# Turning the quantised activations with VectorE blocks and a trip through DRAM, where TensorE transposed them

## The reference

```python
def fp4_quant_dequant(x):
    xb = x.reshape(shape[:-1] + (shape[-1] // BLOCK, BLOCK))      # BLOCK = 16
    scale = jnp.maximum(jnp.max(jnp.abs(xb), axis=-1, keepdims=True) / 6.0, 1e-12)
    xn = xb / scale
    return (_GRID[jnp.searchsorted(_MID, jnp.abs(xn))] * jnp.sign(xn) * scale).reshape(shape)

gate, y = fp4_linear(x, w_gate), fp4_linear(x, w_up)              # 256 -> 704
return fp4_linear(jax.nn.silu(gate) * y, w_down)                  # 704 -> 256
# whole: x + attn(xn) + ffn(xn), xn = layernorm(x)
```

## Time and profile before

| | |
|---|---|
| median of three runs | 2815.54 us |
| the profiled execution: its time | 2811.82 us |
| its span, first to last instruction | 2810.2 us |
| PE busy | 2577.6 us, 92% |
| ACT busy | 2034.4 us, 72% |
| DVE busy | 1936.9 us, 69% |
| POOL busy | 687.3 us, 24% |
| granted TensorE clock, mean | 0.970 |

### The profile page before, as it was taken

How to read it: one execution, slowest core, us unless ns; L and a number is a source line. 1 busy time by engine, 2 the same in 40 slices (tenths; PEclk the granted TensorE clock), 3 DMA queues, 4 the chain that set the end, 5 groups by cost and what they waited for, 6 DMA issues and landing times.

```text
span 2810.2 us, 60356 instructions
## 1 busy us (share of the span) xinstructions
PE 2577.6 (92%) x18236; PEld 1313.6 (47%) x18236; DVE 1936.9 (69%) x5533; ACT 2034.4 (72%) x3510; POOL 687.3 (24%) x478
## 2 busy tenths in 40 slices
PE   2995998898889859999999999999999999999999
PEld 1883444444444424444454445445444445444445
DVE  6895998898889865656655665655566564656555
ACT  1554887897889857777766777775777775777775
POOL 3563233323232212111111211211121121212211
PEclk8997999999999989999999999999999999999999
DMA  2785544444454442122123022031221231220200
GB/s 68 234 269 119 78 61 67 69 67 69 67 70 67 62 78 45 32 33 46 28 63 72 22 41 47 22 69 58 33 49 26 34 69 54 45 47 22 41 24 31
DMA packets 117099, 175.52 MB, mean 62 GB/s; under 512 B 24880, under 2 KB 93232, under 8 KB 116272
## 3 DMA queue, kind: packets, MB, share of 16 engines
q1 hardware_dynamic: 97392, 147.33, 27.9%
q10 hardware_dynamic: 16576, 15.73, 2.1%
q0 software_dynamic: 2816, 8.91, 1.1%
HBM read 129.37 MB, written 42.53 MB: 61 GB/s over the span
## 4 chain that ended last, share of the span: by engine, by line
PE 53%; ACT 4%; issue 4%; DMA 1%; SPq 1%; DVE 0%; ACTq 0%; POOL 0%; DVEq 0%; POOLq 0%
PE O L918 17%; PE S L902 15%; PE F L938 10%; PE F L978 5%; ACT probs L1047 4%; PE F L968 2%; PE S L989 2%; PE S L905 2%; SPq L528 1%; PE F L931 1%; DMA y<-in_L_attn_x_dram 1%; DMA q_st<-s_shift 0%; ACTq L1042 0%; DVE o_turned L1253 0%; DVE ht_lo L1241 0%
## 5 line engine op out<-in xcount | busy, mean ns | idle before, releaser
L1047 ACT ACTIVATE probs<-S 128x1024 f32<-128x1024 f32 (+3 forms) x1280 | 1074.7, 897 | 213.7 <-PE S L902 77.3
L744 DVE CUSTOM_DVE_ANT_0 m_excess<-m_S,m_excess 128x512 f32<-128x512 f32 (+7 forms) x1536 | 702.3, 531 | 58.8 <-ACT m_excess L723 38.3
L723 ACT ACTIVATE m_excess<-m_DIFF 128x512 f32<-128x512 f32 (+7 forms) x1536 | 640.5, 473 | 124.8 <-PE m_DIFF L676 36.1
L902 PE MATMUL S<-q_st,k_st 128*128 128x512 bf16 (+3 forms) x2560 | 648.3, 351 | 65.7 <-DMA q_st<-s_shift 28.7
L918 PE MATMUL O<-probs,v_sb 128*32 128x512 f32 (+3 forms) x5120 | 602.3, 542 | 1.7 <-POOL v_sb L1124 1.7
L676 PE MATMUL m_DIFF<-m_k,m_q_diff 128*128 128x512 bf16 (+7 forms) x1536 | 489.9, 326 | 61.0 <-DMA m_q_diff<-s_q 29.8
L676 PE MATMUL m_S<-m_k,m_q 128*128 128x512 bf16 (+7 forms) x1536 | 492.1, 330 | 18.5 <-DVE m_row_max L744 10.6
L902 PEld LDWEIGHTS S<-q_st,k_st 128*128 128x128 bf16 x2560 | 213.4, 98 | 407.8 <-ACT probs L1047 236.3
L631 POOL TENSOR_TENSOR m_q_diff<-m_zero,m_q 48x4096 bf16<-48x4096 bf16 x32 | 224.3, 7011 | 519.6 <-DMA m_q<-s_q 508.5
L676 PEld LDWEIGHTS m_S<-m_k,m_q 128*128 128x128 bf16 x1536 | 150.4, 98 | 257.5 <-DVE m_row_max L744 181.3
L1241 DVE TENSOR_TENSOR ht_lo<-F,ht_hi 128x512 fp32r<-128x512 f32 (+1 forms) x128 | 71.0, 558 | 232.0 <-ACT ht_hi L1062 232.0
(11 more groups left out here) (163 smaller groups left out, 4167.9 us busy)
## 6 DMA issues: line engine op xcount, KB each, us to landing
k_st<-s_k SPq DMA_DIRECT2D x96, 256.0 KB, 8.5
q_st<-s_q SPq DMA_DIRECT2D x384, 64.0 KB
s_q<-a_part SPq DMA_DIRECT2D x48, 256.0 KB, 3.0
s_k<-a_part SPq DMA_DIRECT2D x48, 256.0 KB, 2.2
m_q<-s_q SPq DMA_DIRECT2D x96, 128.0 KB, 3.6
m_k<-s_k SPq DMA_DIRECT2D x96, 128.0 KB, 6.4
m_q_diff<-s_q SPq DMA_DIRECT2D x96, 128.0 KB, 7.9
m_k<-s_k SPq DMA_DIRECT2D x96, 124.0 KB, 5.1
```

The source lines that it names most:

```text
L723: act.activation(excess[u % MAX_EXCESS][:, 0:keys // 2], DIFF[u % MAX_BUFS][:, 0:keys // 2], ACT.Relu) \
L744: dve.tensor_tensor_reduce(larger, S[u % MAX_BUFS][:, 0:keys // 2], larger, 1.0, -3e38, ALU.add, ALU.max, column).then_inc(reduced[u % MAX ...
L902: ins = pe.matmul(S[half][:, s % 2, 0:st.width], k_st[p][:, s, st.j * P:(st.j + 1) * P], q_st[st.c % 2][:, s, st.skip:QC], start=True, sto ...
L1047: act.activation(probs[half][st.n % 2][:, :, 0:st.width], S[half][:, :, 0:st.width], ACT.Exp, scale=SCALE).then_inc(exped[half], 1)
```

## The change

Four edits, all in the main phase.

1. The turns. The transposes on PE (`x_turn`, `h_turn`) go. DVE transposes `x_fp4` and `h_fp4` in 32x32 blocks with one instruction each, into `x_flip` and `h_flip` (`h_flip` is also the buffer of `h_norm`). SP stores that to DRAM (128x256 and 128x768 float32), waits for the store, and loads it back with `unflip`: four DMAs, each for 32 partitions, whose contiguous pieces are 32 floats (128 bytes). That puts each block in its place, so `xt` and `ht` in SBUF are the transposed tiles.
2. ACT makes `xt_hi` at k=0 and `ht_hi` at k=9, now one instruction of 768 columns, from SBUF. POOL makes `xt_lo` and `ht_lo`.
3. SP's program is written out for the whole batch, with its loads in the order of the steps: the load of q for the next chunk stands where a chunk begins, ahead of `turn_h` where both are at k=4. The loads of the next batch's first tiles and v come at the end of a batch, v last.
4. After the steps: `h_turn` on DVE at m=2, `down` at m=12. At a batch's start `place_v` on POOL stands behind `x_rescale`.

```diff
-GATED_AT = {0: ("turn", 0), 2: ("gate", 0), 3: ("up", 0), 5: ("gate", 1), 6: ("up", 1)}
-GATED_FIRST_AT = {2: ("turn", 0), 4: ("gate", 0), 5: ("up", 0), 7: ("gate", 1), 8: ("up", 1)}
+GATED_AT = {0: ("high", 0), 2: ("gate", 0), 3: ("up", 0), 5: ("gate", 1), 6: ("up", 1)}
+GATED_FIRST_AT = {2: ("high", 0), 4: ("gate", 0), 5: ("up", 0), 7: ("gate", 1), 8: ("up", 1)}
+def unflip(eng, dst, dram, tiles, sem):
+    blocks = dram.rearrange("(a r) (m g s) -> g r m a s", r=SLOT, s=SLOT, g=P // SLOT)
+    for g in range(P // SLOT):
+        rows = dst[g * SLOT:(g + 1) * SLOT, :].rearrange("r (m a s) -> r m a s", m=tiles, s=SLOT)
+        eng.dma_start(rows, blocks[g]).then_inc(sem, 16)
+UNFLIP_DMAS = P // SLOT
...
+            def load_chunk(b, chunk):
+                hg, c = divmod(chunk, NQC)
+                if c == 0:
+                    load_stack(sp, k_st[hg % 2][:, :, :], dram["k"], K_STACK, hg * HG, HG, bass.ds(b * T, T), group_ld[hg % 2])
+                q = q_st[c % 2]
+                tokens = bass.ds(b * T + c * QC, QC)
+                sp.wait_ge(q_zeroed, 2)
+                sp.wait_ge(o_free[c % 2], b * (chunks // 2) + chunk // 2 + PRIMED)
+                load_stack(sp, q[:, :, :], dram["q"], Q_STACK, hg * HG, HG, tokens, q_ld[c % 2])
+                sp.dma_start(q[STACK:QK_ROWS, :, :],
+                             dram["shift"][:, bass.ds(b * H + hg * HG, HG), c * QC:(c + 1) * QC]) \
...
+                sp.wait_ge(q_zeroed, 2)
+                sp.wait_ge(v_ready, b * NHG + PRIMED)
+                sp.dma_start(v_in[:, :, :], dram["v"][:, bass.ds(b * NKB, NKB), :]).then_inc(v_ld, 16)
+            def turn_x(b, n):
+                sp.wait_ge(q_zeroed, 2)
+                sp.wait_ge(x_flipped, b * tiles + n + 1 + PRIMED)
+                sp.dma_start(dram["x_flip"], x_flip[:, :]).then_inc(x_flip_st, 16)
+                sp.wait_ge(q_zeroed, 2)
+                sp.wait_ge(x_flip_st, b * (16 * tiles) + 16 * (n + 1) + PRIMED)
+                unflip(sp, xt, dram["x_flip"], KD, xt_ld)
+            def turn_h(b, n):
+                sp.wait_ge(q_zeroed, 2)
+                sp.wait_ge(h_flipped, b * tiles + n + 1 + PRIMED)
+                sp.dma_start(dram["h_flip"], h_flip[:, :]).then_inc(h_flip_st, 16)
+                sp.wait_ge(q_zeroed, 2)
+                sp.wait_ge(h_flip_st, b * (16 * tiles) + 16 * (n + 1) + PRIMED)
+                unflip(sp, ht, dram["h_flip"], ITILES, ht_ld)
+            def batch(b, more):
+                turn_x(b, 0)
+                for st in steps:
+                    n, k = divmod(st.n, per_tile)
+                    if st.first and st.chunk + 1 < chunks:
+                        load_chunk(b, st.chunk + 1)
+                    if k == 4 and n >= 1:
+                        turn_h(b, n - 1)
+                    elif k == 6 and n + 1 < tiles:
+                        turn_x(b, n + 1)
+                if more:
+                    load_chunk(b + 1, 0)
+                turn_h(b, tiles - 1)
+                if more:
+                    load_batch(b + 1)
...
+            def down(b, n):
+                pe.wait_ge(ht_lo_done, b * tiles + n + 1 + PRIMED)
+                if n + 1 < tiles:
+                    pe.wait_ge(gated_done, b * 2 * tiles + 2 * (n + 2) + PRIMED)
                 else:
-                    pe.wait_ge(gate_free, b * 2 * tiles + 2 * n + 1 + PRIMED)
-                gated_product(0, "gate", ch, gate_ps)
...
                     if k == 0 and n >= 2:
                         down(b, n - 2)
-                    if op == "turn":
-                        x_turn(b, n)
-                    elif op == "gate":
+                    if op == "gate":
                         gate(b, n, ch)
                     elif op == "up":
                         up(b, n, ch)
-                    elif k in (8, 9) and n >= 1:
-                        h_turn(b, n - 1, k - 8)
                 down(b, tiles - 2)
                 values(b, steps[-1])
                 for m in range(tiles):
-                    if m == FLUSH_TURN:
-                        for part in range(2):
-                            h_turn(b, tiles - 1, part, flush=True)
-                    elif m == FLUSH_DOWN:
+                    if m == FLUSH_DOWN:
                         down(b, tiles - 1)
                     project(b, m)
...
+            def x_high(b, n):
+                act.wait_ge(xt_ld, b * (16 * UNFLIP_DMAS * tiles) + 16 * UNFLIP_DMAS * (n + 1) + PRIMED)
+                act.wait_ge(up_ps, b * 2 * tiles + 2 * n + PRIMED)
+                act.activation(xt_hi[:, :], xt[:, :], ACT.Copy).then_inc(xt_hi_done, 1)
+            def h_high(b, n):
+                act.wait_ge(ht_ld, b * (16 * UNFLIP_DMAS * tiles) + 16 * UNFLIP_DMAS * (n + 1) + PRIMED)
+                act.wait_ge(down_ps, b * tiles + n + PRIMED)
+                act.activation(ht_hi[:, :], ht[:, :], ACT.Copy).then_inc(ht_hi_done, 1)
             with act.Fori(0, B) as b:
                 for st in steps:
                     op, ch = gated_op(n, k)
                     exps(b, st, 0)
                     exps(b, st, 1)
-                    if op == "turn":
-                        act.wait_ge(xt_ps, b * tiles + n + 1 + PRIMED)
-                        act.activation(xt_hi[:, :], F[0][:, 0:KD * P], ACT.Copy).then_inc(xt_hi_done, 1)
+                    if op == "high":
+                        x_high(b, n)
                     elif op == "gate":
                         gate_parts(b, n, ch)
-                    elif k in (8, 9) and n >= 1:
-                        h_high(b, n - 1, k - 8)
+                    if k == 9 and n >= 1:
+                        h_high(b, n - 1)
                     if k == 9 and n + HEAD_TILES < tiles:
                         if n == 0:
                             act.wait_ge(y_st, b * (16 * (len(STORES) - 1)) + PRIMED)
                         load_tile(b, n + HEAD_TILES)
-                for part in range(2):
-                    h_high(b, tiles - 1, part)
+                h_high(b, tiles - 1)
                 for first, last in STORES:
                     store(b, first, last)
             act.wait_ge(y_head_st, 16 * B + PRIMED)
...
+            def x_low(b, n):
+                pool.wait_ge(xt_hi_done, b * tiles + n + 1 + PRIMED)
+                pool.tensor_tensor(xt_lo[:, :], xt[:, :], xt_hi[:, :].bitcast(F32), ALU.subtract).then_inc(xt_lo_done, 1)
+            def h_low(b, n):
+                pool.wait_ge(ht_hi_done, b * tiles + n + 1 + PRIMED)
+                pool.tensor_tensor(ht_lo[:, :], ht[:, :], ht_hi[:, :].bitcast(F32), ALU.subtract).then_inc(ht_lo_done, 1)
...
                 x_rescale(b, 0)
+                place_v(b, 0)
                 for st in steps:
                     n, k = divmod(st.n, per_tile)
+                    if gated_op(n, k)[0] == "high":
+                        x_low(b, n)
                     if k == 1:
                         add_bias(b, n)
                         if n + 1 < tiles:
                         x_rescale(b, n + 1)
                     elif k == 8:
                         h_normalise(b, n)
+                    elif k == 9 and n >= 1:
+                        h_low(b, n - 1)
                     if st.c == NQC - 1 and st.j == NKB // 2 and st.hg + 1 < NHG:
                         place_v(b, st.hg + 1)
                 h_rescale(b, tiles - 1)
+                h_low(b, tiles - 1)
...
+                def x_turn(n):
+                    dve.wait_ge(x_ready, b * tiles + n + 1 + PRIMED)
+                    dve.wait_ge(xt_lo_done, b * tiles + n + PRIMED)
+                    dve.transpose(x_flip[:, :], x_fp4[:, :]).then_inc(x_flipped, 1)
+                def h_turn(n):
+                    dve.wait_ge(h_ready, b * tiles + n + 1 + PRIMED)
+                    dve.wait_ge(ht_lo_done, b * tiles + n + PRIMED)
+                    dve.transpose(h_flip[:, :], h_fp4[:, :]).then_inc(h_flipped, 1)
...
                 x_scales(0)
                 x_round_(0)
+                x_turn(0)
                 for st in steps:
                     n, k = divmod(st.n, per_tile)
                     if k == 0:
                         if n >= 2:
                             add_down(n - 2)
-                        x_low(n)
                     elif k == 1 and n + 1 < tiles:
                         x_scales(n + 1)
                     elif k == 2 and n >= 1:
                         h_round_(n - 1)
                     elif k == 3:
                         gate_chunk(n, 0)
-                    elif k == 4 and n + 1 < tiles:
-                        x_round_(n + 1)
+                    elif k == 4:
+                        if n + 1 < tiles:
+                            x_round_(n + 1)
+                        if n >= 1:
+                            h_turn(n - 1)
                     elif k == 6:
                         gate_chunk(n, 1)
+                        if n + 1 < tiles:
+                            x_turn(n + 1)
                     elif k == 7:
                         h_scales(n)
```

(11 more changed lines are left out.)

114 lines of the change are left out of this document (35 added, 79 removed).

## The result

The changed kernel takes 2971.66 us (median; the kernel before beside it 2816.18): ratio 1.0552, 95% interval 1.0536 to 1.0568, so 155 us slower. The forecast was 2868, 52 slower. Its profiled span is 2958.3 us against 2810.2.

What follows compares the result with a forecast made beforehand. The prediction took PE to bound the kernel, with 1.18 us of transposes a tile on its path. 2811.8 us, +35 inside batches and +18 between them gave 2865, or 2868 for the median; range 2808 to 2990.

Steps and rivals of the forecast that it cites:

- the gain of h's turn: At `down`: k=9's scores start 0.59 us earlier, but the gain is spent on the low part, leaving x's 0.22.
- r=0: Tiles with n mod 4 = 0: q's load stands ahead of h's trip, so `down` is late; +0.8 us each.
- r=2: Tiles with n mod 4 = 2: h's trip stands behind q's load, `ht` 2.1 us late; +2.0 us each.
- The low part: Before `down`: ACT's copy 0.80, POOL's subtraction 1.51 and handovers 0.15, so 2.45 us behind k=9's last exponential.
- r=1 and 3: Tiles with n mod 4 = 1 or 3, no q load at k=4: `ht` in time with 2 us to spare, -0.2 us each.
- The four together: Tiles inside batches, by n mod 4: costs and gains sum to +8.8 us a batch, +35 over four batches.
- Between batches: Joints, first start and last end: 5.0 us at each of three joints, about +1 and +1.7 at the ends; +18.
- Rival A: DRAM trips: 128-byte pieces slow or ring full, a trip 8.7 us or more; 2920, or beyond 2990; chance 0.28.
- B: DRAM trips: always hidden; 2818 if all are, 2842 at a trip of 6.1 us; chance 0.13.
- C, the other side: At `down`: ACT so far ahead that h's parts finish during `values`, so the gain stays; 2774 us; chance 0.10.
- D: At `down`: something else paces it, as the q load at tile 4, absorbing lateness; within the forecast's range; chance 0.04.
- The start of the reading: Chain of waits over the whole span: nearly all PE, the transposes that go 3% of it, ACT's exponentials 4%.

Runs made afterwards that it cites:

- e5: Changed kernel with q of chunk 1 loaded before x's first trip, the last h turned once rounded, x turned before the gate: 2922.3 us.
- e1: Changed kernel without the trips through DRAM, DVE's transposes writing `xt` and `ht` directly, blocks not put in place: 2855.6 us.
- e17: Changed kernel loading the same bytes back from DRAM in whole rows instead of 128-byte pieces, blocks not put in place: 2924.8 us.
- e3: Changed kernel without the trips through DRAM (blocks not put in place) and with the low parts on DVE instead of POOL: 2801.6 us.
- e4: Changed kernel with SP doing h's trip ahead of the chunk load where both are at k=4: 3091.0 us.
- e16: Against the kernel before: only x by DVE and DRAM, low part on DVE, starts reordered, k's load behind q's at k=2, next batch's loads early: 2865.2 us.
- e19: As e16, but k, q and norm issued at k=0 of tiles with n mod 4 = 3, v at k=4 of tile 15: 2818.2 us.
- e12: Against the kernel before: only x goes by DVE and DRAM, its low part on POOL; PE turns h as before: 2923.3 us.
- e18: Changed kernel, low parts on DVE, SP and DVE reordered, some `ht_hi` at k=8, next batch's loads early, k's load at k=0 of every fourth tile: 2851.3 us.

## Why the prediction was wrong in size

- Direction and the mechanism inside a tile hold: the gain of h's turn is waited out, q stands ahead of the trip at k=4, and ACT waits for `ht` at r=0, and slightly at r=2. L968 and L931 are gone, `down` waits for `ht_lo` in nearly every tile.
- The low part: 2.86 us from `ht` to `down`, not 2.45. It was scaled from a row of POOL with one broadcast operand, and two full ones took 1.85. The copy was 0.85 for 0.80. So tiles with r=1 and 3 cost +0.48 and +0.25 and not -0.2: some 15 us.
- r=0: +3.1 and not +0.8. The trip was 0.5 longer and the low part 0.4, but the main error is that I read the deadline in tile 4 of the second batch, where the kernel before itself stood for its q load: that interval was 27.2 us, and 26.0 in tiles 8 and 12. From the end of the rounding to the end of k=9's exponentials it has 11.8 us, and they have 9.8 and 10.3.
- r=2: +0.8 and not +2.0, again by the tile that was read. In tile 14 the changed SP has no q load ahead of the trip, as no chunk is left, and it takes 26.76 us in every batch, +0.4. And in tile 14 the time from the end of DVE's rounding to the end of k=9's exponentials was 10.5 us, where tiles 2, 6 and 10 have 11.6 to 11.8. In tile 10 of the second batch `ht` was 0.2 us late and not 2.1:

```profile
1830.31 0.84 ACT L1087 ACTIVATE ht_hi<-ht 128x768 fp32r<-128x768 f32 x1 [0.19 <-DMA ht<-s_h_flip]
```

- The four together are 4.7 us and not 2.4 for four tiles.
- Between batches, the step that failed: +18 forecast, 88 measured. It counted x's trip, `place_v` and the turn of the last h as if each began when its data was ready, and priced a transfer and never what it stands behind. It left out that the next batch's k and v go out 80 us later (v 1431.88 to 1511.11), that q of chunk 1 is behind x's trip, that the last h waits on DVE for more than the 1.0 us it was given, and the clock at 1.2 GHz around these waits. e5 gave 44 of it back by three moves of order. e1, without the trips, gave back 17.3 a joint and 6.2 and 6.1 at the two ends, 64 us, and 46 inside the batches. What the clock costs by itself was not separated; the 37 us above are an estimate for the whole run.
- Rival A (small pieces): true in kind, 48 us by e17, a third of the loss. Its trip of 8.7 us or more is not what ran (median 7.7), and that its 2920 lies nearer to 2972 than 2868 does is not to its credit: it has the joints at 22. B: wrong. C, the other side: even with the trip free and the low part short the kernel is at 2802, not 2774. D: the q load did pace tile 4.
- The start of the reading: 3% and 4% are shares of the span, and not of the chain, which is 63% of it; the transposes are nearer 5% of the chain. No term of the sum rests on it.
- The rule on pieces under 512 bytes, in the Trainium skill, DMA: Bandwidth & Descriptors, Specifications: the forecast said that the row of 64-byte pieces shows no such price. That was too quick, since nothing in the trace before had the same bytes in large pieces. Side by side, 128-byte pieces cost 0.25 us more to issue and 0.7 more to land for 96 KB. The price agrees with the rule; the reason that the page gives, no run tests. The forecast's second estimate, from the skill's fit in Anatomy of one DMA, had 2.9 us for the store and 2.33 were measured; the page gives that fit for DMAs that GpSimd issues, and these are SP's.

## What to carry to other kernels

A trip through DRAM costs no more than its latency only where the queue is empty. Before pricing one, write down for each of its issues what stands ahead of it on its sequencer and what is in flight on the DMA engines: here a load of 1.5 MB made a store that else lands in 1.7 to 3.7 us take 10 to 13. Then look at what now stands behind it; an engine that ran ahead of the work (SP, prefetching a batch's k and v over 50 us early) loses that when it is given a wait in every step. Read a deadline in more than one place: tiles 4 and 14, the two that the forecast read, were both unlike their kind. And taking work off the busiest engine is worth no more than what the others don't wait out: of 71 us, 25 arrived inside the batches and 12 in the whole when all else was taken away (e3).

## What the runs showed of the hardware

- A store of 128 KB issued right behind six loads of 256 KB took 10.3 to 13.1 us (twelve times in e4; 10.4 to 12.9 in e16), against 1.7 as the median where nothing is ahead (e19). A 128 KB load from another engine's queue took 7.7 to 14.3 (twelve times in e12), against 2.1 as the median.
- A store issued 11 us after the first of k's six DMAs, with q and norm behind them, was still held up: 7.3 us to the first load and not 2.4 (e18).
- A load of 96 KB in 128-byte pieces: 0.65 us to issue, 2.9 to land; in rows of 3072 bytes 0.4 and 2.2 (e17).
- 128x768 float32, two full operands in SBUF: POOL 1.81 us, DVE 0.96. Where POOL's met a DVE instruction of two such operands (128x704, 0.89 us alone), they took 2.45 and 2.37.
- DVE's transpose in 32x32 blocks, 768 columns: 0.97 us.
